# Reordered loads, rests, sums and gates in steps 0 and 1 of two feed-forward stages, and of turned norms and probabilities in the last attention unit

## The reference, cut to what matters

```python
x = x + 0.5 * ffn(layernorm(x))        # x: 2 x 512 tokens, 512 wide, float32
x = x + attention(layernorm(x))        # 32 query heads, 8 key/value heads, head size 128, causal, ALiBi bias
x = x + 0.5 * ffn(layernorm(x))        # the same weights again
...
def ffn(x):                            # each weight is w * (su @ sv), rank 4
    a = x @ (gate_w * (gate_su @ gate_sv)).T      # 1792 wide
    b = x @ (up_w * (up_su @ up_sv)).T
    return (silu(a) * b) @ (down_w * (down_su @ down_sv)).T
```

## Time and profile before

| what | value |
|---|---|
| median of three runs | 1282.38 us (1280.07 to 1282.55) |
| the profiled execution, its own time | 1279.44 us |
| its span, first to last instruction | 1278.1 us |
| TensorE matmuls busy | 1243.2 us, 97% of the span |
| VectorE, ScalarE, GpSimd busy | 809.6, 732.9 and 526.2 us |
| DMA | 60.20 MB, mean 47 GB/s |
| granted TensorE clock | 1.000 |

### The profile page before, as it was taken

How to read it: one execution, slowest core, us unless ns; L and a number is a source line. 1 busy time by engine, 2 the same in 40 slices (tenths; PEclk the granted TensorE clock), 3 DMA queues, 4 the chain that set the end, 5 groups by cost and what they waited for, 6 DMA issues and landing times.

```text
span 1278.1 us, 18363 instructions
## 1 busy us (share of the span) xinstructions
PE 1243.2 (97%) x6562; PEld 1058.0 (83%) x6562; DVE 809.6 (63%) x1978; ACT 732.9 (57%) x1738; POOL 526.2 (41%) x412
## 2 busy tenths in 40 slices
PE   5999999999999999999999999999999989999999
PEld 4777888788888888888888888888888777788887
DVE  7866666675656666566566566666656767655555
ACT  3544443257657667667666667667667674444442
POOL 5586551634224324315315314313413344575550
PEclk9999999999999999999999999999999999999999
DMA  6043222101001001001101001001001010121101
GB/s 224 36 139 118 102 101 99 51 1 50 34 1 50 34 1 50 34 1 50 34 1 50 34 1 51 34 1 50 34 1 50 11 40 1 51 69 64 50 17 66
DMA packets 15018, 60.20 MB, mean 47 GB/s; under 512 B 2064, under 2 KB 2736, under 8 KB 12880
## 3 DMA queue, kind: packets, MB, share of 16 engines
q1 hardware_dynamic: 14544, 58.47, 13.0%
q10 hardware_dynamic: 384, 0.56, 0.1%
HBM read 45.91 MB, written 13.11 MB: 46 GB/s over the span
## 4 chain that ended last, share of the span: by engine, by line
PE 90%; DVE 4%; ACT 2%; issue 2%; POOL 1%; DMA 1%; SPq 0%; DVEq 0%; ACTq 0%
PE bank L284 27%; PE bank L285 27%; PE bank L286 27%; PE bank L479 5%; PE bank L458 2%; PE bank L312 1%; DVE mix_l L1024 1%; PE bank L461 1%; DVE mix L1015 1%; ACT prob L790 0%; ACT prob L799 0%; DVE probT_l L1169 0%; DVE raw_early L926 0%; DMA x_rows<-x 0%; POOL w_l_early L1254 0%
## 5 line engine op out<-in xcount | busy, mean ns | idle before, releaser
L1332 POOL TENSOR_TENSOR rows<-rows,row_root_y 128x640 f32<-128x640 f32 x64 | 80.6, 1259 | 272.0 <-DVE row_root_y L892 272.0
L790 ACT ACTIVATE prob<-prob,neg_top 128x128 f32<-128x128 f32 (+3 forms) x256 | 141.0, 552 | 75.8 <-DVE neg_top L1158 75.2
L1326 POOL TENSOR_TENSOR square<-rows 128x640 f32<-128x640 f32 x64 | 80.3, 1254 | 205.5 <-ACT rows L769 205.5
L805 ACT CAST probT_h<-bank 128x512 fp32r<-128x512 f32 x160 | 84.5, 596 | 136.9 <-PE bank L479 136.9
L799 ACT ACTIVATE prob<-prob,inverse 128x128 f32<-128x128 f32 (+3 forms) x256 | 122.9, 554 | 1.8 <-DVE inverse L1163 1.8
L284 PE MATMUL bank<-w_h_late,xnT_hi 128*128 128x512 f32 (+1 forms) x352 | 121.2, 344 | 0.0
L286 PE MATMUL bank<-w_h_late,xnT_lo 128*128 128x512 f32 (+1 forms) x352 | 118.6, 337 | 0.0
L285 PE MATMUL bank<-w_l_late,xnT_hi 128*128 128x512 f32 (+1 forms) x352 | 118.3, 336 | 0.0
L1254 POOL TENSOR_TENSOR w_l_late<-raw_late,w_h_late 128x512 fp32r<-128x512 f32 (+1 forms) x58 | 88.5, 1545 | 69.4 <-ACT w_h_late L585 69.4
L1169 DVE TENSOR_TENSOR probT_l<-bank,probT_h 128x512 fp32r<-128x512 f32 x160 | 101.6, 685 | 21.9 <-ACT probT_h L805 21.7
L1183 DVE TENSOR_TENSOR x_rows<-bank,x_rows 128x512 f32<-128x512 f32 x64 | 44.2, 690 | 105.0 <-PE bank L286 105.0
(11 more groups left out here) (175 smaller groups left out, 3510.3 us busy)
## 6 DMA issues: line engine op xcount, KB each, us to landing
raw_late<-w_qkv SPq DMA_DIRECT2D x8, 1536.0 KB, 6.3
raw_early<-ffn_w SPq DMA_DIRECT2D x21, 512.0 KB, 3.8
scaled<-raw_early SPq DMA_DIRECT2D x21, 512.0 KB, 2.6
raw_late<-scaled SPq DMA_DIRECT2D x21, 512.0 KB, 3.6
raw_late<-w_o SPq DMA_DIRECT2D x8, 1024.0 KB, 4.8
y<-x_rows SPq DMA_DIRECT2D x8, 256.0 KB, 2.0
x_rows<-x SPq DMA_DIRECT2D x6, 256.0 KB, 5.2
x_rows<-x ACTq DMA_DIRECT2D x2, 256.0 KB, 4.3
```

Of the source, the lines that this page charges most:

```text
L790: last = act.activation(p, p, ACT.Exp, bias=neg_top[:, h:h + 1], scale=-1.0, accum_out=total[:, h:h + 1])
L805: act.copy(probT_h[:, j, :, :], banks[r.bank][:, :].rearrange("p (h q) -> p h q", h=G)).then_inc(probT_hi_done, 1)
L1326: pool.tensor_tensor(square[:, n % 2, :, :], row, row, ALU.mult).then_inc(squares_done, 1)
L1332: pool.tensor_tensor(row, row, by, ALU.mult).then_inc(rows_normed, 1)
```

## The change

Ten reorderings, none of which adds or removes an arithmetic instruction:

- Start: SyncE loads `fix_raw` and x blocks 0, 1 and 2 in that order; ScalarE issues `lo_rows` and the factor tile first and x block 3 last. GpSimd waits for the four normed tiles (`xn_done`) after the rests of `fix` and `fac_gu0`, before the other two factor rests and the second half of `fix`.
- `whole_tokens(0)` waits for the second `d_lo` of batch 0 in step 0, as `whole_tokens(1)` already does.
- `ffn_first`: from the turned norms of batch 1 on, TensorE's rotation is banks 2 to 7.
- `ffn_first`: VectorE takes the rest of mix 0 before mix 3, and the rest of the last gate before the rests of mixes 2 and 3. ScalarE casts mixes 2 and 3 together after the last gate; with p = 1 it splits a11 and a12 of step 1 before the cast of the gate's product.
- `ffn_second(0)`: product 5 goes ahead of the scale of `down`.
- `stack_ahead(2)`: earlier on ScalarE (ahead of `silu_of(p, 1, 1, 0)`) and on GpSimd (ahead of the splits of step 2); its three factor loads are issued by SyncE ahead of the weights of step 2.
- p = 1: GpSimd splits a11 and a12 of step 1 before all weight sums, and makes s3 and s4 after the rests of s1 and s2.
- Last unit: ScalarE and VectorE read norms 0 and 1, then the probabilities, then norms 2 and 3; VectorE adds the output of unit 62 last. TensorE's order there stays.

```diff
@@ -364,6 +364,7 @@
             def ffn_first(p):
                 gate_up(p, 0, 1, 0)
+                rotation[0] = range(2, BANKS)
                 turn_normed(2 * p, 1)
                 down(p, 0, 0)
                 gate_up(p, 0, 0, 1)
@@ -378,9 +379,9 @@
                 product(p, 1, 1)
                 product(p, 1, 2)
                 down(p, 0, 1)
+                product(p, 1, 5)
                 if p == 0:
                     scale_weights(1, "down")
-                product(p, 1, 5)
                 product(p, 1, 6)
                 if p == 0:
                     scale_weights(2, "gu0")
@@ -546,10 +547,9 @@
         def scalar_program():
             def load_first():
-                for t in range(2, TB):
-                    act.dma_start(xr[:, t, :], x_rows[t]).then_inc(x_in[t], 16)
                 act.dma_start(lo_rows, factor_lo).then_inc(fix_in, 16)
                 act.dma_start(fac_raw["gu0"], ffn_fac[0, 0]).then_inc(fac_in["gu0"], 16)
+                act.dma_start(xr[:, TB - 1, :], x_rows[TB - 1]).then_inc(x_in[TB - 1], 16)
             def stack_factors(s, kind):
                 act.wait_ge(fac_in[kind], 16 * (s + 1))
@@ -652,13 +652,15 @@
                         stack_factors(1, kind)
                 mix_hi(p, 0)
                 gate(p, 0, 0, 1)
-                mix_hi(p, 1, 2)
+                mix_hi(p, 1)
+                if p == 1:
+                    split(p, 1, "a11", "a12")
                 gated_hi(p, 0, 0, 1)
-                split(p, 1, "a11", "a12")
-                if p == 0:
+                if p == 0:
+                    split(p, 1, "a11", "a12")
                     stack_factors(2, "gu0")
                 gate(p, 0, 1, 1)
-                mix_hi(p, 3)
+                mix_hi(p, 2, 3)
                 gated_hi(p, 0, 1, 1)
                 if p == 0:
                     stack_factors(2, "gu1")
@@ -682,13 +684,13 @@
                 partial_sum(p, 1, 7, 0)
                 silu_of(p, 1, 1, 1)
                 partial_sum(p, 1, 7, 1)
+                if p == 0:
+                    stack_ahead(2)
                 silu_of(p, 1, 1, 0)
                 product_hi(p, 1, 1, 1)
                 split(p, 2, "a11")
                 product_hi(p, 1, 1, 0)
                 split(p, 2, "a12")
-                if p == 0:
-                    stack_ahead(2)
             def ffn_step(p, s):
                 after = s + 1 < STEPS
@@ -798,8 +800,8 @@
                     p = prob[:, h, 0:keys]
                     act.activation(p, p, ACT.Copy, scale=inverse[:, h:h + 1]).then_inc(prob_done, 1)
-            def turn_probabilities(n):
-                for j in range(unit(n)[2] + 1):
+            def turn_probabilities(n, blocks=None):
+                for j in blocks or range(unit(n)[2] + 1):
                     r = results["turn_prob", n, j]
                     act.wait_ge(full[r.bank], r.nth)
                     act.copy(probT_h[:, j, :, :], banks[r.bank][:, :].rearrange("p (h q) -> p h q", h=G)).then_inc(probT_hi_done, 1)
@@ -833,8 +835,10 @@
                 if g < HKV - 1 and at == LEAD - 1:
                     split_qkv(g + 1, range(AHEAD, KC))
                 if n == UNITS - 1:
-                    turn_normed(2, 0)
+                    turn_normed(2, 0, (0, 1))
                 turn_probabilities(n)
+                if n == UNITS - 1:
+                    turn_normed(2, 0, (2, 3))
                 if at == 0:
                     split_o(g, (0, 1))
@@ -1036,15 +1040,18 @@
                 down(p, 0, 0)
                 if p == 1:
                     mix_tokens(p, 0)
-                mix_tokens(p, 2, 1, 3)
+                mix_tokens(p, 2, 1)
+                mix_lo(p, 0)
+                mix_tokens(p, 3)
                 gated_up(p, 0, 0, 1)
                 if p == 0:
                     scale_weights(1, "gu0")
                 gated_lo(p, 0, 0, 1)
-                mix_lo(p, 0, 1)
-                gate_up(p, 0, 1, 1)
+                mix_lo(p, 1)
+                gated_up(p, 0, 1, 1)
                 if p == 0:
                     scale_weights(1, "gu1")
+                gated_lo(p, 0, 1, 1)
                 mix_lo(p, 2, 3)
             def ffn_second(p):
@@ -1211,10 +1218,13 @@
                 if n + LEAD < UNITS:
                     values_lo(n + LEAD)
                 if n == UNITS - 1:
-                    turn_normed(2, 0)
-                if n:
+                    turn_normed(2, 0, (0, 1))
+                elif n:
                     project_out(n - 1)
                 turn_probabilities(n)
+                if n == UNITS - 1:
+                    turn_normed(2, 0, (2, 3))
+                    project_out(n - 1)
             for t in range(TB):
                 dve.wait_ge(x_in[t], 16)
@@ -1289,10 +1299,7 @@
             def whole_tokens(p):
-                if p == 0:
-                    pool.wait_ge(xn_done, 2 * TB)
-                else:
-                    pool.wait_ge(d_done, gate_nth(1, 0, 1, 0) + 1)
+                pool.wait_ge(d_done, gate_nth(p, 0, 1, 0) + 1)
                 r = results["xn", 2 * p, 0, TB - 1]
                 pool.wait_ge(evac[r.bank], r.nth)
                 for k, at in ((0, 0), (2, 3)):
@@ -1359,21 +1366,17 @@
                 if p == 0:
                     for kind in KINDS:
                         stack_factors(1, kind)
-                else:
-                    mix_weights(p, 1)
                 split(p, 1, "a11", "a12")
                 if p == 0:
                     stack_factors(2, "gu0")
                     stack_factors(2, "gu1")
-                if p == 0:
-                    mix_weights(p, 1, second=False)
+                mix_weights(p, 1, second=False)
                 split(p, 1, "s1", "s2")
-                if p == 0:
-                    mix_weights(p, 1, first=False)
+                mix_weights(p, 1, first=False)
                 split(p, 1, "s3", "a22", "s4", "d0", "d1")
+                if p == 0:
+                    stack_ahead(2)
                 split(p, 2, "a11", "a12")
-                if p == 0:
-                    stack_ahead(2)
                 mix_weights(p, 2)
                 for s in range(2, STEPS):
                     after = s + 1 < STEPS
@@ -1402,6 +1405,8 @@
             pool.wait_ge(fix_hi, 1)
             rest(fix[:, 0:DM], fix_raw[:, 0:DM], fix[:, 0:DM]).then_inc(fix_lo, 1)
             stack_factors(0, "gu0")
+
+            pool.wait_ge(xn_done, TB)
             stack_factors(0, "gu1")
             pool.wait_ge(fix_hi, 2)
             rest(fix[:, DM:2 * DM], fix_raw[:, DM:2 * DM], fix[:, DM:2 * DM]).then_inc(fix_lo, 1)
@@ -1481,9 +1486,9 @@
                 sp.wait_ge(qkv_lo, (g + 1) * KC)
                 sp.dma_start(late_room[0][:, 0:G * DM], w_o[g]).then_inc(w_in["o"], 16)
-            for t in range(2):
+            sp.dma_start(fix_raw, ffn_fix).then_inc(fix_in, 16)
+            for t in range(TB - 1):
                 sp.dma_start(xr[:, t, :], x_rows[t]).then_inc(x_in[t], 16)
-            sp.dma_start(fix_raw, ffn_fix).then_inc(fix_in, 16)
             load_ffn(0, "gu0")
             for kind in KINDS[1:]:
                 sp.dma_start(fac_raw[kind], ffn_fac[0, KINDS.index(kind)]).then_inc(fac_in[kind], 16)
@@ -1507,15 +1512,19 @@
                     load_factors(2, "gu1")
                     keep_scaled(1, "gu0")
                     keep_scaled(1, "gu1")
+                    load_factors(3, "gu0")
+                    load_factors(3, "gu1")
+                    load_factors(2, "down")
                 load_ffn(s + 1, "gu0")
                 load_ffn(s + 1, "gu1")
                 if s == 1:
                     keep_scaled(s, "down")
                     load_ffn(s + 1, "down")
-                if seven(0, s + 1):
-                    load_factors(s + 2, "gu0")
-                    load_factors(s + 2, "gu1")
-                load_factors(s + 1, "down")
+                if s > 1:
+                    if seven(0, s + 1):
+                        load_factors(s + 2, "gu0")
+                        load_factors(s + 2, "gu1")
+                    load_factors(s + 1, "down")
                 keep_scaled(s + 1, "gu0")
                 keep_scaled(s + 1, "gu1")
                 if s > 1:
```

More of the change, by code:

```diff
@@ L1367, in ffn @@
                     stack_factors(2, "gu1")
-                if p == 0:
-                    mix_weights(p, 1, second=False)
+                mix_weights(p, 1, second=False)
                 split(p, 1, "s1", "s2")
-                if p == 0:
-                    mix_weights(p, 1, first=False)
+                mix_weights(p, 1, first=False)
                 split(p, 1, "s3", "a22", "s4", "d0", "d1")
-                split(p, 2, "a11", "a12")
                 if p == 0:
                     stack_ahead(2)
+                split(p, 2, "a11", "a12")
                 mix_weights(p, 2)
```

## The result

The changed kernel takes **1268.37 us** in the median (1267.37 to 1268.68, five runs), the kernel before 1282.38 (1280.07 to 1282.55, five runs): a ratio of 0.9898 with an interval of 0.9887 to 0.9909, 14.0 us less. Forecast were 1271.1 us and 11.3 less. From one profiled execution to the other it is 1279.44 to 1268.68, 10.8 less. These two differences are not the same number, and most of the story is in why.

A forecast was written before the change was run, and what follows sets the result against it. TensorE's matmuls were taken as busy for 97% of the span, leaving only its waits, some 35 us. Terms sum to 11.3: profiled 1279.4 to 1268.1, plus 2.9 to the median's base, 1271.1 us; range 1266.5 to 1277.

The forecast's parts named there:

- start: Up to the first gate: root chain 3.5 us shorter, x 0.45 later; 3.0 us less (bounds 1.5 to 3.5).
- whole_tokens(0): Step 0, before the first down: both d_lo at 0.69 without GpSimd's sums beside them; 1.4 us less (0.6 to 1.9).
- product 5, `stack_ahead(2)`: Steps 1 and 2: scale of down no longer waits, 0.7 us less; step 3's weights come earlier, 1.5 less.
- last unit: Last weighted values: their 2.30 us wait for the first probabilities shrinks; 1.7 us less (1.0 to 2.2).
- banks, split, p = 1: Product 1, step 1, second FFN: reserved banks remove its second half's wait, 2.2 us; earlier split its first's, 0.8.
- Rival (b): Start: a slow TensorE runs the first gate at half rate for up to 3 us, losing 1.5; 1272.6 us, chance 0.08.
- (a): All terms: the next wait takes part of each, leaving half the sum; 1276.5 us, chance 0.21.
- (c): First FFN's opening: TensorE held long at half rate, gain gone from fifty matmuls on, 1287 us at 72; chance 0.04.
- (d): Nothing measurable: brackets overlap, a stall removed early reappears at the next load (step 3's weights); 1281 us, chance 0.05.

The follow-up runs named there:

- c4: The changed kernel without the reserved banks: 1268.59 us (four runs), ratio 0.9904 to the kernel before.
- a4: The kernel before with only whole_tokens(0) moved later, to wait for the second rest of batch 0: 1281.42 us, ratio 0.9998.
- c2: The changed kernel with idle matmuls, seven between the first scale and the turns and four ahead of the first gate: 1267.12 us, ratio 0.9892.
- c1: The kernel before with idle matmuls in four of TensorE's pauses: 1279.97 us over ten runs, ratio 0.9988.
- a2: The kernel before with only the start's new order of loads: 1280.48 us, ratio 0.9990.
- b4: The kernel before with only stack_ahead(2), its loads, and product 5 ahead of the scale of down: 1277.64 us, ratio 0.9965.
- a3: The kernel before with only GpSimd's wait at the start, loads as before: 1279.63 us, ratio 0.9989.
- a1: The kernel before with the start's order of loads and GpSimd's wait together: 1277.27 us, ratio 0.9968.
- b3: The kernel before with only the last unit's order of readings changed: 1279.82 us in nine runs, ratio 0.9984.
- b1: The kernel before with only the reserved banks (rotation of banks 2 to 7 in ffn_first): 1278.95 us, ratio 0.9981.
- b2: The kernel before with only the new order of mixes, gates, splits and weight sums, eight banks as before: 1277.17 us, ratio 0.9965.
- c3: The changed kernel with four idle matmuls ahead of the first gate alone: 1266.70 us (four runs), ratio 0.9889.

## Why the prediction was right, and where not

The direction and the range held, and each edit shortened the wait that it aimed at. The table above, column c4, is the test of the sum at the full clock, since the execution that I reckoned from had it too:

| term | forecast | at full clock | from the table |
|---|---|---|---|
| start | 3.0 | 3.08 | first gate |
| `whole_tokens(0)` | 1.4 | 1.35 | 4.43 - 3.08 |
| product 5, `stack_ahead(2)` | 0.7 + 1.5 | 2.66 | 7.09 - 4.43 |
| last unit | 1.7 | 1.58 | 8.43 - 6.85 |
| banks, split, p = 1 | 2.2 + 0.8 | 3.28 (without the banks) | 11.71 - 8.43 |
| sum | 11.3 | 11.95, less 0.24 lost in between | |

**Start.** Right to 0.1 us: the root chain, its 3.5 us (measured 3.4) and the 0.45 for the later x (the second root step starts 0.41 later). That loads and wait move the gate by 0.4 and 2.0 alone and by 3.0 together follows from the same mechanism.

**`whole_tokens(0)`.** Right at the full clock, 1.35. Missed: a fall in the first gate hides the same wait. In an execution of the kernel before with that fall the wait is 0.53 already, the term is not there, and a4 shows no gain in its median.

**Step 2 and product 5.** Mis-sized by half a microsecond; 2.66 in c4, and the same 2.66 in after. The three brackets account for 0.74 + 0.72 + 0.64 (1.61 to 0.97) = 2.1 of it. The rest is a term that the sum left at nothing: a pause costs more than its bracket. TensorE before, around the wait of 0.72:

```profile
91.36 0.39 PE L286 MATMUL bank<-xnT_hi,w_l_early 128*128 128x512 f32 x1
92.47 0.50 PE L284 MATMUL bank<-mix_h,mixed_h 128*128 128x512 f32 x1 [0.72 <-POOL mixed_l L1254]
92.80 0.39 PE L285 MATMUL bank<-mix_l,mixed_h 128*128 128x512 f32 x1
```

In a dense row starts lie 0.23 apart, here 1.11 and 0.33: 0.98 us are lost, 0.26 more than the bracket shows. Two such pauses gone make 0.52, and 2.1 + 0.52 = 2.62. Of the 1.61 about 1.0 stays, a little more than the 0.8 I left out of reach.

**Banks and split at p = 1.** The sum of 3.0 was right, the sharing out was not. The step that failed is the treatment of 2.2 and 0.8 as independent. The text even noted that "`d` itself also comes earlier", and gave that no number: it comes early enough to take all but 0.4 of the wait by itself. The order of the weights gives 3.28 of the 3.67 that the changed kernel gains here (10.72 - 7.05), the reserved banks the last 0.4, which four runs of c4 can't tell from nothing. The two brackets were 3.09 in all, and with 0.26 more for each pause that makes 3.61 of the 3.67.

**Last unit.** 1.58 in c4, 1.57 in after, against 1.7.

**Rival (b)** has its size right (1.5; measured 1.6, in the profiled execution and, by their clock, in three of the changed kernel's five runs), and its place, but not its mechanism; that the number fits is luck. It supposed a slow start that ends at a time and so reaches into the earlier gate. The slow start has no end of that kind and reached the gate in no profile: it was over at 10.74 behind seven matmuls more (c2), and in kernels with the same work there at about 14.4 (the changed one) or only at 16.4 (c4). And the execution that lost the 1.6 had been fast before the pause and fell. I took the loss for something that the change might bring in. In fact the kernel before had such falls at four places, only not in the execution whose trace I read.

**The base.** That is the real error. I read "2.9 below the median" as a constant offset and moved the whole forecast by it. It was falls of the clock (c1): the profiled execution had none, the median run, by its time, two. Since they follow pauses and the change shortens or removes the pauses at three of the four places, most of them go. At 1.000 against 1.000 the gain is 1279.7 - 1267.4 = 12.3; in the medians of the first five runs each 14.0, as the kernel before pays for about two falls there and the changed one for at most one. Forecast from 11.3 and one fall less, the number would have been near 1269.6.

**Rivals (a), (c) and (d)**: no removed wait reappeared later with a bracket over 0.3 us (the first gate's own grew by 0.6, as the scale ahead of it ran faster), no long stretch at half rate came, and the measured ratio is clear of one. Two of the prediction's sums are off without touching the forecast: all terms at their upper bound and 1.5 more give 1267.4, not 1266.5, as the lower end of the range, and half the sum gives 1276.7, not 1276.5, for (a).

## What to carry to other kernels

Before a median is predicted from one profiled execution, sort the runs by their granted clock: if they fall into steps, the offset between profile and median belongs to events at places, and an edit there changes it; what such an event costs depends on the waits behind it. Where two edits aim at neighbouring waits of one engine, list for each what the other one already moves, and try both alone and without each; here one of them could nearly be left out. A pause that can't be removed may be filled with idle matmuls, if it is TensorE's and just ahead of dense work; four of them were worth more than the reserved banks. And a bracket of TensorE's timeline is the lower bound of what its pause costs: compare the distances of starts.

## What was unexpected of the hardware

- The granted clock fell to 0.50 for 3 to 4 us behind pauses of TensorE of 1.8 to 2.3 us in otherwise dense work, in some executions and not in others. In the profiled executions without filling the wait before the first gate was 1.22 or 1.23 us (before, a2, b4, c4) and 1.42 (a3) where none followed, and 1.83, 1.84, 2.18, 2.20, 2.22 and 2.25 (after, a1, b3, a4, b1, b2) where one did. The longer wait is no cause by itself: it is longer because the scale ahead of it was fast (four matmuls in 0.72 to 0.82 us, against 1.20). So what goes with the fall is TensorE being fast before the pause. Yet the kernel before went through waits of 1.89, 2.30 and 2.25 at its other places without one. A fall takes 1.6 us, of which a wait behind it can take up nearly all (b1). With matmuls in the pauses it happened in none of 18 runs (c1, c2, c3). The Trainium skill, TensorE: Matmul & The Clock Gate, section The HAM clock gate, says that "the default state is throttled, and activity releases the throttle"; the filled kernels agree with it. Which pause brings a fall in which execution no run here settles.
- The first sixteen turns run at half rate (3.62 us against 1.94 behind seven idle matmuls) under a granted clock that the profile gives as 1.00 in both.
- Tiny VectorE instructions suffer most from GpSimd's: a root step on 128x4 took 0.73 us beside a rest on 32 partitions and 0.16 without it. In the kernel before GpSimd's rests ran from 7.82 to 12.35, and in that time VectorE got through five root steps, each ending within 0.05 us of a rest's end: 4.3 us for what takes 0.8 alone. That is the whole of 5.42 - 1.99 = 3.4 us.
